# Dst-order passes of a four-layer graph network on blocks of 128 nodes in place of 256

## The chip, the core and the metric

One core of a Trainium2 chip runs the whole kernel. The metric is the device time of one execution in microseconds; the program before was timed in three runs. Five engines work beside each other, each through its own list of instructions in order: PE (TensorE), DVE (VectorE), ACT (ScalarE), POOL (GpSimd) and SP (SyncE), and they meet by semaphores. "PEld" is the weight load of TensorE, which the profile lists apart from the matmul.

## The reference

A graph of 6250 nodes (128 features each, f32) and 100000 edges, which are sorted by `dst` on entry. Four layers are applied, each to a normalized copy `h` of `x`, and added to `x`:

```python
edge_index = jnp.stack([src, dst])
h = jnp.maximum(_layernorm(x, axis=-1), 0.0)
x = x + _L0_gnn_ref(src, edge_type_200, dst, h, ...)       # 3 sums over edges by src, weighted; then softmax over all edges, sum
h = jnp.maximum(_layernorm(x, axis=-1), 0.0)
x = x + _L1_gnn_ref(h, edge_index, W, att_src, att_dst, bias)   # GAT: 8 heads, softmax over the edges of one dst, sum by dst
h = jnp.maximum(_layernorm(x, axis=-1), 0.0)
x = x + _L2_gnn_ref(h, edge_index, edge_attr_128, ...)     # segment_sum(x_nei[src] + edge_attr @ W.T, dst) / degree
h = jnp.maximum(_layernorm(x, axis=-1), 0.0)
x = x + _L3_gnn_ref(h, edge_index, edge_type_2, ...)       # segment_sum(one of two linear maps of X[src] by type, dst)
```

The work that counts is the segment sums: 128 floats of each of 100000 edges are added to the row of the edge's node, three times by `src` with a weight (layer 0), once more by `src` with the softmax, and by `dst` for `edge_attr`, the GAT layer, the mean layer and the typed layer.

## The kernel before

**A step.** A pass goes over the edges in tiles of 128. One step fetches the 128 rows of its tile, builds a one-hot matrix (128 edges x 256 nodes of a window, true where the edge's node is that column), and multiplies: PE has the fetched rows (128 x 128) as weights and the one-hot as the moving operand, and leaves 128 features x 256 nodes in PSUM. DVE adds that to the window's columns in an accumulator that holds all nodes (25 windows of `WN` = 256 columns). The number of the window is read from a table into a register for each step, so a tile lies in one window alone; where a window ends inside a tile the edges are tiled again from there. A pass has about 781 tiles of edges and some for the windows: 806 to 816 steps.

**The passes in order, with their place in the profiled execution** (us from the span's start):

- Preparation, to 346. DVE counts edges by window with one pass over all edge keys for each of the 25 windows (L458), works out where each tile starts (L497 and L499, a pair of operations for each window), and waits for records that POOL has scattered.
- ATTR, 346 to 1196, 808 steps in dst order. SP loads the rows of `edge_attr` by plain DMA (L1810). Meanwhile POOL scatters one record for each edge to put the edges into src order, 800 indirect DMAs (L1675).
- A normalization, then S0, S1, S2 from 1379 to 4943, 806 steps each in src order with weights, and SCORES, 5030 to 6276, in src order. From here on POOL fetches the rows of each step by an indirect DMA (a gather, L1696; L1712 in SCORES) into a ring of 16 tiles (33 in SCORES).
- GAT, 6468 to 7922, dst order, 816 steps in 51 groups of 16, ring of 48 tiles, gathers L1724.
- MEAN, 8015 to 9289, dst order, 808 steps; every 16 steps one extra product of 128 nodes is made (`own_term`: three matmuls L1177 to L1179 on PE, L582 and L584 on DVE).
- TYPED, 9429 to 10600, dst order, 808 steps; then the output.

**A step of the row passes** (ATTR, S0 to S2, MEAN, TYPED; `sum_pass` on DVE and on PE). DVE builds the one-hot `OH` (L604, or L601 with a weight) up to four steps ahead, and two instructions later adds the product of the step before last (L613). PE (L1184) waits for the one-hot, for the gathered rows and for the add that frees its PSUM bank. One f32 matmul is two MATMUL records and two LDWEIGHTS records in the trace. POOL (L1696) waits for `s_mm` of sixteen steps before, then issues its gather; nothing else stands in its queue.

**A step of GAT.** DVE makes the one-hot in bf16 (L991); PE transposes its two halves (L1356, L1357); ACT copies the transposed form out (L1574); PE looks up the attention terms of the edges' nodes by two matmuls of 24 columns (L1370). For each group of 16 steps a chain of 26 small DVE operations, seven PE steps and some on ACT works out the running maximum of each node and a factor by which old sums are rescaled (`rescale`, L981 and L983, once a group). ACT copies the one-hot to f32 (L1584), DVE multiplies the gathered rows by the attention (L998), PE forms the sums with the one-hot's halves as weights and the rows (146 columns: 128 features and 18 sums) as moving operand (L1380, L1381), and DVE adds 292 columns to the accumulator (L1014). The lookup side runs 33 steps ahead of the sums (`LAG1`), each engine's list being written out step by step in one loop.

Of the kernel before, what the change touches and what calls it, by code (L numbers as in the profile page):

```python
# [5 lines left out]
ALU = mybir.AluOpType  # L6
ACT = mybir.ActivationFunctionType
F32 = mybir.dt.float32
BF16 = mybir.dt.bfloat16
# [15 lines left out]
NTL = (E + NW * 142) // 128  # L25
# [7 lines left out]
NL1 = 816  # L33
# [18 lines left out]
def program(nc, x, src, dst, edge_attr_128, edge_type_2, edge_type_200,  # L52
# [5 lines left out]
    with ctx:  # L58
# [129 lines left out]
        def slot(k, dt=I32):  # L188
            v = RA[0:EP, k * EC:(k + 1) * EC]
            return v if dt is F32 else v.bitcast(dt)  # L190
# [19 lines left out]
        cnt1 = ST[:, 352:352 + NW]  # L210
# [36 lines left out]
        NER, NBR, NBB, KLR = RC[0:1, 1408:2224], RC[0:1, 2224:3040], RC[0:1, 3040:3856], WE0[0:1, 0:816]  # L247
        TR17, V17 = ST[0:1, 0:136], ST[0:1, 136:272]
        F17 = [ST[0:1, 272:408], ST[0:1, 408:544]]
        CFR = RC[0:1, 3856:3984]  # L250
        TRB, VBR = OH[0:1, 3, 0:128], OH[0:1, 3, 128:256]
        FBR, CBR = WE0[0:1, 0:128], WE0[0:1, 128:256]
        OHR, OHN = WE0[0:1, 256:512], WE0[0:1, 512:768]
        R18, DR = ST[0:1, 544:562], ST[0:1, 562:570]
        F18 = ST[:, 576:612].rearrange("p (a k) -> p a k", k=18)
# [48 lines left out]
        def window(e, regs, tab, t):  # L304
            if t % 16 == 0:
                e.load(regs, tab[0:1, t:t + 16])  # L306
            return e.snap(regs[t % 16], min_val=0, max_val=NW - 1)
# [4 lines left out]
        def _(v):  # L312
# [138 lines left out]
            tot1, nt1, cum1, st1, sh1 = (ST[:, 384 + 32 * k:384 + 32 * k + NW] for k in range(5))  # L451
            v.tensor_scalar(wi, slot(1), 8, None, ALU.arith_shift_right).then_inc(prep.sem, prep.one())
# [3 lines left out]
            for b in range(NW):  # L456
# [5 lines left out]
            v.tensor_copy(tot1, PS[2][:, 0:NW]).then_inc(prep.sem, prep.one())  # L462
            ti, al1 = SI[:, 8:8 + NW], ST[:, 592:592 + NW]
            own_done(prep)
            v.tensor_tensor_scan(st1, ONES[:, 0:NW], tot1, 0.0, ALU.mult, ALU.add).then_inc(prep.sem, prep.one())
            own_done(prep)
            v.tensor_copy(ti, st1).then_inc(prep.sem, prep.one())
            own_done(prep)
            v.tensor_scalar(ti, ti, 4, 4, ALU.arith_shift_right, ALU.logical_shift_left).then_inc(prep.sem, prep.one())
            own_done(prep)  # L470
            v.tensor_copy(al1, ti).then_inc(prep.sem, prep.one())
            v.tensor_copy(nt1[:, 0:1], st1[:, 0:1]).then_inc(prep.sem, prep.one())
            own_done(prep)
            v.tensor_tensor(nt1[:, 1:NW], st1[:, 1:NW], al1[:, 0:NW - 1], ALU.subtract).then_inc(prep.sem, prep.one())
            own_done(prep)
            v.tensor_scalar(ti, nt1, 127.0, None, ALU.add).then_inc(prep.sem, prep.one())
            own_done(prep)
# [1417 lines left out]
```

## Time and profile before

| | us |
|---|---|
| runs of the kernel before, median (lowest, highest) | 10542.12 (10536.25, 10543.48) |
| the profiled execution | 10618.11 |
| its span | 10616.3 |
| PE busy, PEld busy | 6277.0, 3729.0 |
| DVE busy | 6150.0 |
| POOL busy | 6440.6 |
| ACT busy | 1211.9 |
| DMA moved | 486.58 MB, mean 46 GB/s |

The profiled execution has its own time, 0.7% over the median. "Busy" is the time in which an engine executes; PE and PEld overlap. No engine is busy for more than 61% of the span, and a share of the whole is a mean over ten stages that differ, so the rows further on are read pass by pass.

### The profile page before, as it was taken

How to read it: one execution, taken by the hardware profiler on the slowest of the kernel's cores; microseconds unless marked ns; L12 is line 12 of the kernel's file. 1: busy time of each engine (PE TensorE's matmuls, PEld its weight loads, DVE VectorE, ACT ScalarE, POOL GpSimd, SP SyncE). 2: the span in 40 equal slices, each digit the busy share in tenths (PEclk: the TensorE clock that was granted, in tenths of full speed). 3: DMA queues.
4: the chain of work that ended last, by engine and by line, in shares of the span. 5: the costliest groups of instructions: out<-in, count | busy, mean ns of one | idle time of the engine just before them, and what ended most of it. 6: DMA issues, size and time to landing. Idle time of an engine off the chain costs nothing. (4 is left out here: it accounts for less than half of the span.)

```text
span 10616.3 us, 114972 instructions
## 1 busy us (share of the span) xinstructions
PE 6277.0 (59%) x20679; PEld 3729.0 (35%) x20679; DVE 6150.0 (58%) x20621; ACT 1211.9 (11%) x3342; POOL 6440.6 (61%) x6535
## 2 busy tenths in 40 slices
PE   0577446666555565555666666777764444575555
PEld 0233222223333333333333334666652333343333
DVE  6666457776545445555666675666675444434444
ACT  0000000000000000001333333444430000010000
POOL 3777766665666656665566635555545656536665
PEclk9988667667666666667666666777776777766666
DMA  2223211112111121112111111111111111211112
GB/s 40 52 63 64 58 39 45 45 46 53 46 46 46 46 54 46 46 46 52 42 43 43 43 39 40 39 40 40 40 26 59 43 42 43 41 48 46 46 46 54
DMA packets 392309, 486.58 MB, mean 46 GB/s; under 512 B 134290, under 2 KB 297942, under 8 KB 391350
## 3 DMA queue, kind: packets, MB, share of 16 engines
q0 software_dynamic: 206816, 377.82, 15.2%
q1 hardware_dynamic: 181770, 99.99, 3.3%
q8 instruction: 201, 3.29, 0.1%
q14 instruction: 502, 4.11, 0.1%
q10 hardware_dynamic: 3020, 1.36, 0.1%
HBM read 443.16 MB, written 37.86 MB: 45 GB/s over the span
## 5 line engine op out<-in xcount | busy, mean ns | idle before, releaser
L1184 PE MATMUL PS<-OH,RING 128*128 128x256 f32 x9684 | 3937.6, 537 | 2834.0 <-DVE OH L604 992.3
L1184 PEld LDWEIGHTS PS<-OH,RING 128*128 128x128 f32 x9684 | 2100.7, 251 | 4659.7 <-DVE OH L601 1525.6
L1696 POOL DMA_INDIRECT RING<-TAB,IDX x2418 | 2315.4, 958 | 1252.9 <-issue 626.4
L613 DVE TENSOR_TENSOR RA<-RA,PS 128x256 f32 x2418 | 1007.7, 417 | 1432.3 <-PE PS L1184 584.6
L613 DVE TENSOR_TENSOR RB<-RB,PS 128x256 f32 x2424 | 1018.8, 420 | 1109.9 <-PE PS L1184 443.0
L1712 POOL DMA_INDIRECT RING<-TABQ,IDX x806 | 784.1, 973 | 549.3 <-PE PS L1270 246.4
L1675 POOL DMA_INDIRECT REC<-RC x800 | 953.7, 1192 | 254.5 <-issue 242.5
L1696 POOL DMA_INDIRECT RING<-TABM,IDX x808 | 769.7, 953 | 543.6 <-issue 200.8
L1696 POOL DMA_INDIRECT RING<-TABN,IDX x808 | 768.1, 951 | 540.5 <-PE PS L1184 244.2
L601 DVE TENSOR_SCALAR OH<-IOTA,KEY,WE 128x256 f32<-128x256 f32 x2418 | 1023.9, 424 | 102.8 <-ACT RA L1492 45.7
L1270 PE MATMUL PS<-OH,RING 128*128 128x256 f32 x1612 | 759.6, 600 | 411.6 <-ACT OH L1516 234.7
L1724 POOL DMA_INDIRECT RING<-TABG,IDX x544 | 536.4, 986 | 540.9 <-PE PS L1381 310.2
L1270 PEld LDWEIGHTS PS<-OH,RING 128*128 128x128 f32 x1612 | 360.3, 272 | 753.7 <-ACT OH L1516 475.6
L604 DVE TENSOR_SCALAR OH<-IOTA,KEY 128x256 f32<-128x256 f32 x1616 | 579.8, 359 | 36.8 <-issue 36.7
L1014 DVE TENSOR_TENSOR RB<-RB,PS 128x292 f32 x816 | 370.1, 454 | 270.2 <-PE PS L1381 233.9
L1516 ACT ACTIVATE OH<-OHB,SC 128x256 f32<-128x256 bf16 x806 | 408.2, 506 | 769.0 <-DVE OHB L763 520.4
L712 DVE SCALAR_TENSOR_TENSOR RC<-IOTA,KEY,RB 128x256 f32<-128x256 f32 x806 | 386.3, 480 | 153.6 <-issue 101.9
L1574 ACT ACTIVATE OHT<-PS 128x256 bf16<-128x256 bf16 x816 | 312.3, 383 | 864.2 <-PE PS L1357 710.4
L776 DVE TENSOR_TENSOR RA<-RA,PS 128x256 f32 x732 | 303.5, 415 | 175.7 <-issue 132.1
L1724 POOL DMA_INDIRECT RC<-TABG,IDX x272 | 265.7, 977 | 226.2 <-PE PS L1381 143.6
L1380 PE MATMUL PS<-RING,OH 128*128 128x146 f32 x1088 | 355.9, 419 | 47.1 <-ACT OH L1584 24.1
L573 DVE SCALAR_TENSOR_TENSOR RC<-IOTA,SC,RELB 128x200 f32<-128x200 f32 x806 | 337.4, 419 | 0.0
(371 smaller groups left out, 6427.8 us busy)
## 6 DMA issues: line engine op xcount, KB each, us to landing
RING<-in_edge_attr_dram SPq DMA_DIRECT2D x808, 64.0 KB
RING<-TAB,IDX POOLq DMA_INDIRECT x2418
RING<-TABN,IDX POOLq DMA_INDIRECT x808
RING<-TABM,IDX POOLq DMA_INDIRECT x808
RING<-TABQ,IDX POOLq DMA_INDIRECT x806
REC<-RC POOLq DMA_INDIRECT x800
TAB<-HN SPq DMA_DIRECT2D x18, 512.0 KB, 3.4
RING<-TABG,IDX POOLq DMA_INDIRECT x544
```

Source lines behind the costliest of these rows:

```text
L601: v.tensor_scalar(OH[:, t % 4, :], IOTA[:, :], key[:, t:t + 1], WE0[:, t:t + 1], ALU.is_equal, ALU.mult).then_inc(s_oh, 1)
L604: v.tensor_scalar(OH[:, t % 4, :], IOTA[:, :], key[:, t:t + 1], None, ALU.is_equal).then_inc(s_oh, 1)
L613: v.tensor_tensor(sl, sl, PS[k % 4][:, 0:WN], ALU.add).then_inc(s_ad, 1)
L712: v.scalar_tensor_tensor(out=junk[:, t % 2, :], in0=IOTA[:, :], scalar=KEY0[:, t:t + 1], in1=PB[:, bass.ds(w * WN, WN)], op0=ALU.is_equal, ...
L1014: v.tensor_tensor(sl, sl, PS[a % 3][:, 0:292], ALU.add).then_inc(s_ab, 1)
L1184: t_.matmul(PS[t % 4][:, 0:WN], GD[:, t % 16, :], OH[:, t % 4, :], start=True, stop=True).then_inc(s_mm, 1)
L1270: t_.matmul(PS[a % 4][:, 0:WN], RG0[:, a % (3 * GS), 0:128], OH[:, a % 4, :], start=True, stop=True).then_inc(s_mm0, 1)
L1516: a_.activation(OH[:, a % 4, :], OHB[:, a % 4, :], ACT.Copy, scale=S0[:, a:a + 1]).then_inc(s_oh0, 1)
L1675: p.indirect_dma_start(REC0, bass.IndirectOffsetOnAxis(ap=posi0[:, c:c + 1], axis=0), v0[:, c:c + 1], None).then_inc(s_put[c % 8], 16)
L1696: p.indirect_dma_start(GD[:, t % 16, :], None, table, bass.IndirectOffsetOnAxis(ap=idx[:, t:t + 1], axis=0)).then_inc(s_ring[t % 16], 16)
L1712: p.indirect_dma_start(RG0[:, s, :], None, TABQ, bass.IndirectOffsetOnAxis(ap=IDX0[:, t:t + 1], axis=0)).then_inc(s_ring[t % 16], 16)
L1724: p.indirect_dma_start(rows_of(t)[:, 0:136], None, TABG, bass.IndirectOffsetOnAxis(ap=IDX1[:, t:t + 1], axis=0)).then_inc(s_ring[t % 16], 16)
```

## The change

All passes in dst order (ATTR, GAT, MEAN, TYPED) take blocks of 128 nodes (`ND` = 49 blocks of `WD` = 128) in place of 25 windows of 256. The src-order passes keep their windows of 256.

- Steps: ATTR, MEAN and TYPED 808 to 830, GAT 816 to 832 (52 groups of 16). Tiles are cut at multiples of 128 edges now, and a tile in which a block ends is fetched again for the next block.
- In a row pass the one-hot, the matmul's moving operand and the add are 128 columns wide.
- In GAT a step has one transpose, one lookup matmul, one product matmul; the copies by ACT, the add (146) and the rescaling (128 + 18) are half as wide, and a factor needs two matmuls for four.
- In the preparation DVE counts 49 blocks for 25 windows, and the starts of tiles come from seven counting operations in place of 24 pairs.

```diff
+ND = 49
+WD = 128
-NTL = (E + NW * 142) // 128
+NTL = 830
-NL1 = 816
+NL1 = 832
...
-            for b in range(NW):
+            for b in range(ND):
                 v.wait_ge(prep.sem, prep.n)
                 v.tensor_scalar(msk[0], wk, float(b), None, ALU.is_equal, ALU.add,
                                 accum_out=cnt1[0:EP, b:b + 1]).then_inc(prep.sem, prep.one())
...
-            for b in range(1, NW):
-                v.wait_ge(prep.sem, prep.n)
-                v.tensor_scalar(tm, tf, cum1[:, b - 1:b], nt1[:, b - 1:b], ALU.is_ge, ALU.mult).then_inc(prep.sem, prep.one())
-                v.wait_ge(prep.sem, prep.n)
-                v.tensor_tensor(BTF, BTF, tm, ALU.add).then_inc(prep.sem, prep.one())
+            for k in range(NTB):
+                own_done(prep)
+                v.tensor_scalar(steps[:, 0:ND - 1], cum1[:, 0:ND - 1], tf[:, k:k + 1], None, ALU.is_le, ALU.add,
+                                accum_out=W1F[:, k:k + 1]).then_inc(prep.sem, prep.one())
...
-                            v.tensor_scalar(OH[:, t % 4, :], IOTA[:, :], key[:, t:t + 1], None,
+                            v.tensor_scalar(OH[:, t % 4, 0:WD], IOTA[:, 0:WD], key[:, t:t + 1], None,
                                             ALU.is_equal).then_inc(s_oh, 1)
...
-                        sl = acc[:, bass.ds(w * WN, WN)]
-                        v.tensor_tensor(sl, sl, PS[k % 4][:, 0:WN], ALU.add).then_inc(s_ad, 1)
+                        sl = acc[:, bass.ds(w * width, width)]
+                        v.tensor_tensor(sl, sl, PS[k % 4][:, 0:width], ALU.add).then_inc(s_ad, 1)
...
-                    t_.matmul(PS[t % 4][:, 0:WN], GD[:, t % 16, :], OH[:, t % 4, :], start=True, stop=True).then_inc(s_mm, 1)
+                    t_.matmul(PS[t % 4][:, 0:width], GD[:, t % 16, :], OH[:, t % 4, 0:width], start=True, stop=True).then_inc(s_mm, 1)
...
-                    t_.transpose(pb[:, 0:128], OBR[:, t % 51, 0:128], IDENTB[:, :])
-                    t_.transpose(pb[:, 128:256], OBR[:, t % 51, 128:256], IDENTB[:, :]).then_inc(s_tp, 1)
+                    t_.transpose(pb, OBR[:, t % 51, 0:WD], IDENTB[:, :]).then_inc(s_tp, 1)
...
-                    t_.matmul(PS[a % 3][:, 0:146], OH[:, a % 3, 0:128], rows_of(a), start=True, stop=True)
-                    t_.matmul(PS[a % 3][:, 146:292], OH[:, a % 3, 128:256], rows_of(a), start=True, stop=True).then_inc(s_mb, 1)
+                    t_.matmul(PS[a % 3][:, 0:146], OH[:, a % 3, 0:WD], rows_of(a), start=True, stop=True).then_inc(s_mb, 1)
...
-                    v.tensor_tensor(sl, sl, PS[a % 3][:, 0:292], ALU.add).then_inc(s_ab, 1)
+                    v.tensor_tensor(sl, sl, PS[a % 3][:, 0:146], ALU.add).then_inc(s_ab, 1)
```

PE in the steady state of GAT: the lookup and the sums of one step, the transposes of the next, and the chain's matmuls for a factor (L1346 and L1347; AD is the table of attention terms). Before:

```order
L1370 ISA
L1370 MATMUL PS<-AD,OHT 128x24
L1370 ISA
L1370 MATMUL PS<-AD,OHT 128x24
L1380 MATMUL PS<-RING,OH 128x146
L1381 MATMUL PS<-RING,OH 128x146
L1356 MATMUL PS<-IDENTB,RA 128x128
L1357 MATMUL PS<-IDENTB,RA 128x128
L1346 MATMUL PS<-ONES,WE 128x18
L1347 MATMUL PS<-ST,WE 128x18
L1346 MATMUL PS<-ONES,WE 128x18
L1347 MATMUL PS<-ST,WE 128x18
```

and the same place after the change:

```order
L1354 ISA
L1354 MATMUL PS<-AD,OHT 128x24
L1362 MATMUL PS<-RING,OH 128x146
L1342 MATMUL PS<-IDENTB,RA 128x128
L1333 MATMUL PS<-ONES,WE 128x18
L1334 MATMUL PS<-ST,WE 128x18
```

The order of the kinds stays, and each pair is one instruction now. DVE in GAT at the end of a group, where old sums are rescaled (RB is the accumulator, ST the factors), before:

```order
L998 TENSOR_TENSOR RING<-RING 128x128
L894 SCALAR_TENSOR_TENSOR RC<-RC 128x128
L306 TENSOR_LOAD WTAB
L981 ISA
L981 TENSOR_TENSOR RB<-RB,ST 128x2x128
L983 ISA
L983 TENSOR_TENSOR RB<-RB,ST 128x2x18
L1014 TENSOR_TENSOR RB<-RB,PS 128x292
```

and after:

```order
L986 TENSOR_TENSOR RING<-RING 128x128
L882 SCALAR_TENSOR_TENSOR RC<-RC 128x128
L308 TENSOR_LOAD WTAB
L969 ISA
L969 TENSOR_TENSOR RB<-RB,ST 128x128
L971 ISA
L971 TENSOR_TENSOR RB<-RB,ST 128x18
L1002 TENSOR_TENSOR RB<-RB,PS 128x146
```

Nothing moved on DVE here; the same instructions are narrower. In MEAN and TYPED, too, each engine has the same instructions for a step as before.

## Rows read from the trace of the kernel before

**Rows 1.** Windows by pass: length; busy of PE, PEld, DVE, ACT, POOL; clock, DMA share.

```profile
346.00:1196.00 850.00, 595.85 (x1616) 306.81 (x1616) 582.31 (x1617) 0.00 (x0) 676.93 (x569) 0.86 0.30 64
...
5030.00:6276.00 1246.00, 799.53 (x1831) 385.98 (x1831) 856.72 (x3665) 427.00 (x986) 744.82 (x765) 0.65 0.18 42
...
6476.00:7878.00 1402.00, 1098.43 (x7180) 935.60 (x7178) 969.05 (x3662) 588.64 (x1929) 749.38 (x763) 0.75 0.18 39
8028.00:9289.00 1261.00, 624.66 (x1909) 391.33 (x1907) 568.19 (x1710) 0.00 (x0) 758.63 (x799) 0.72 0.17 42
9439.00:10599.00 1160.00, 660.77 (x1616) 359.70 (x1614) 542.93 (x1613) 0.00 (x0) 762.36 (x801) 0.68 0.19 46
```

**Rows 2.** Windows of line L1696 alone, POOL gathers of the MEAN and TYPED passes.

```profile
8015.00:9278.00 1263.00, 768.10 (x808) 0.72 0.18 45
9429.00:10591.00 1162.00, 769.70 (x808) 0.68 0.18 46
```

**Rows 3.** Page, costliest groups: the matmul of the row passes and its weight load.

```profile
L1184 PE MATMUL PS<-OH,RING 128*128 128x256 f32 x9684 | 3937.6, 537 | 2834.0 <-DVE OH L604 992.3
L1184 PEld LDWEIGHTS PS<-OH,RING 128*128 128x128 f32 x9684 | 2100.7, 251 | 4659.7 <-DVE OH L601 1525.6
```

**Rows 4.** Timeline of POOL in TYPED, two pauses; 14 gathers stand between them.

```profile
9879.40 0.95 POOL L1696 DMA_INDIRECT RING<-TABM,IDX  x1 [3.05 <-remote]
...
9899.45 0.95 POOL L1696 DMA_INDIRECT RING<-TABM,IDX  x1 [1.46 <-remote]
```

**Rows 5.** Timeline of DVE in TYPED: two steps of the fast phase, two slow.

```profile
9885.81 0.42 DVE L613 TENSOR_TENSOR RB<-RB,PS 128x256 f32 x1
9886.14 0.35 DVE L604 TENSOR_SCALAR OH<-IOTA,KEY 128x256 f32<-128x256 f32 x1
9886.44 0.42 DVE L613 TENSOR_TENSOR RB<-RB,PS 128x256 f32 x1
...
9891.63 0.42 DVE L613 TENSOR_TENSOR RB<-RB,PS 128x256 f32 x1 [2.15 <-PE PS L1184]
...
9895.12 0.42 DVE L613 TENSOR_TENSOR RB<-RB,PS 128x256 f32 x1 [2.74 <-remote]
```

**Rows 6.** MEAN: waits of the whole run, then timeline of DVE and of POOL.

```profile
DVE HN L582 <- remote: 476.6, 49, 12.2
...
8500.00 0.35 DVE L582 TENSOR_SCALAR HN<-PS,RDEG 128x128 f32<-128x128 f32 x1 [10.12 <-remote]
8500.39 0.29 DVE L584 TENSOR_TENSOR HN<-HN,PS 128x128 f32<-128x128 f32 x1
...
8502.49 0.94 POOL L1696 DMA_INDIRECT RING<-TABN,IDX  x1 [4.87 <-PE PS L1184]
```

**Rows 7.** GAT: windows of line L1014, then groups by form of 6476 to 7878.

```profile
6467.00:7922.00 1455.00, 369.95 (x816) 0.75 0.17 38
...
L1724 POOL DMA_INDIRECT RING<-TABG,IDX x507 | 498.8, 984 | 417.6 <-PE PS L1381 278.3 <-issue 137.9 <-remote 1.4
L1014 DVE TENSOR_TENSOR RB<-RB,PS 128x292 f32 x771 | 349.5, 453 | 263.7 <-PE PS L1381 228.5 <-remote 15.5 <-issue 10.9
...
L991 DVE TENSOR_SCALAR RA<-IOTAB,KEY 128x256 bf16<-128x256 bf16 x770 | 219.1, 285 | 0.1
...
L1380 PEld LDWEIGHTS PS<-RING,OH 128*128 128x128 f32 x1028 | 204.9, 249 | 51.4 <-issue 45.6 <-DVE RING L998 4.4
```

**Rows 8.** ATTR: timeline of SP and of POOL, waits of the whole run.

```profile
700.58 29.13 SPq L1810 DMA_DIRECT2D RING<-in_edge_attr_dram  x27
...
1360.85 1.19 POOL L1675 DMA_INDIRECT REC<-RC  x1 [0.30 <-issue]
...
DVE RC L519 <- DMA RC<-REC: 139.6, 1, 139.6
...
DVE HN L519 <- DMA RC<-RECX,SI: 98.9, 1, 98.9
```

**Rows 9.** Groups by form of DVE before 346 us (preparation).

```profile
L458 DVE TENSOR_SCALAR_CACHE_REDUCE RC<-RING 125x800 f32<-125x800 f32 x25 | 24.6, 986 | 0.9
```

More of the change, by code:

```diff
@@ L448, in _ @@
             v.tensor_copy(TWI[:, 0:NTB], W0F).then_inc(prep.sem, prep.one("tw0"))
-            tot1, nt1, cum1, st1, sh1 = (ST[:, 384 + 32 * k:384 + 32 * k + NW] for k in range(5))
-            v.tensor_scalar(wi, slot(1), 8, None, ALU.arith_shift_right).then_inc(prep.sem, prep.one())
+            tot1, st1, cum1, steps = (ST[:, 64 * k:64 * k + ND] for k in range(4))
+            v.tensor_scalar(wi, slot(1), 7, None, ALU.arith_shift_right).then_inc(prep.sem, prep.one())
             own_done(prep)
@@ new lines, in _ @@
+            for a, b, di in ((0, 33, ti), (33, 48, IOI[:, 0:15])):
+                own_done(prep)
+                v.tensor_copy(di, st1[:, a:b]).then_inc(prep.sem, prep.one())
+                own_done(prep)
+                v.tensor_scalar(di, di, 7, None, ALU.arith_shift_right).then_inc(prep.sem, prep.one())
+                own_done(prep)
+                v.tensor_copy(cum1[:, a:b], di).then_inc(prep.sem, prep.one())
+            own_done(prep)
+            v.tensor_tensor(cum1[:, 0:ND - 1], cum1[:, 0:ND - 1], IOTA[:, 1:ND], ALU.add).then_inc(prep.sem, prep.one())
@@ L470, in _ @@
             own_done(prep)
[L471 to L477, printed above, removed]
-            v.tensor_scalar(ti, ti, 7, None, ALU.arith_shift_right).then_inc(prep.sem, prep.one())
@@ L587, in sum_pass @@
                 n, base = ROW_PASSES[i], before[i]
+                width, blocks = (WN, NW) if weighted else (WD, ND)
                 for t in range(n + 2):
@@ L607, in sum_pass @@
                         k = t - 2
[L608 removed]
+                        w = window(v, regs, tab, k, blocks)
                         v.wait_ge(s_mm, base + k + 1)
@@ L961, in chain_step @@
                         v.wait_ge(s_scaled, c)
-                    v.tensor_copy(ST[:, 576:612], PS[7][:, 416:452]).then_inc(chain.sem, chain.one(("fac", c)))
+                    v.tensor_copy(F18, PS[7][:, 416:434]).then_inc(chain.sem, chain.one(("fac", c)))
             def chain_part(t, part):
@@ L1170, in sum_pass @@
                 n, base = ROW_PASSES[i], before[i]
+                width = WN if SUM0 <= i < SCORES else WD
                 for t in range(n):
```

99 lines of the change are left out of this document (39 added, 60 removed).

## The prediction

> **What bounds the kernel now.** I read the windows by pass first, since no engine is busy for more than 61% of the whole. The reader should see that the four dst-order passes have four different limits.
>
> ATTR [rows 1, 8]: DVE (582 us) and PE (596 us) are busy for some 70% of 850 us. SP issues a load each 29.13/27 = 1.08 us, and 808 steps in 850 us are 1.05 each, so SP's issuing is the pace. It isn't on the path: POOL's scatter of the records runs until 1360.85 + 1.19 = 1362.0, 166 us after ATTR's end at 1196, and S0 can't begin before; DVE waits 139.6 us for the records (`DVE RC L519 <- DMA RC<-REC`).
>
> MEAN and TYPED [rows 1, 2]: 1263/808 = 1.563 and 1162/808 = 1.438 us a step, with DVE and PE busy for about half. POOL's gather takes 0.95 us and 0.30 until the next; 15 of them take 9899.45 - 1.46 - 9879.40 = 18.59 us [rows 4], so call the floor 1.25 us a gather. POOL pauses for 3.05 us once in 15 or so, because it waits for `s_mm` of sixteen steps before: 15 x 1.25 + 3.05 is 21.8 us, or 1.45 a gather, which agrees. The ring is full at such a pause and PE slow: adds come 3.5 us apart (9891.63 to 9895.12), though for the fast phase ahead of them a step takes 9886.44 - 9885.81 = 0.63 us [rows 5]. So PE alternates between a fast phase of about 10 us (9879.40 to 9889.5, where the wait of the slow add begins) and a slow one, in which a step takes 3.5 us with rows and one-hots there. What makes PE slow I can't name; it sets in after POOL has issued without a pause for some time, and ends when POOL pauses. MEAN adds its own terms: DVE waits at L582 49 times, 476.6 us in all, and the POOL pause there is 4.87 us [rows 6].
>
> GAT [rows 1, 7]: 816 adds in 1455 us, 1.783 a step. POOL's gather is 0.984 + 0.30 = 1.29. DVE is busy for 969.05/771 = 1.26 us of each step, PE for 1.42; DVE waits 228.5 us for L1381, which is 0.30 a step. No slow phase of the kind above is to be seen; here the work itself, on DVE and PE in turn, is the limit.
>
> **The change part by part.** The sum is made against the profiled execution of 10618.11 us.
>
> *Preparation and ATTR: 0.* 24 more counts of 0.986 us [rows 9] and their readouts are about 25 us; less L497, which goes (10.8 us in 24), they leave +14 at most. They stand ahead of DVE's wait of 98.9 us for the records of the first scatters [rows 8], which swallows them. ATTR's 22 more steps at 1.05 are +23. Cover: 166 us until the scatter's end. A narrower one-hot doesn't help either, since SP is the pace. Were the cover gone, it would cost up to 37 us. Bounds 0 and 0.
>
> *GAT.* DVE: L1014 goes from 292 to 146 columns. An operation of this kind takes 0.42 us at 256 columns [rows 5] and 0.29 at 128 (L584, rows 6), which makes about 0.31 at 146, -0.145 from 0.453. L991 at 0.285 for 256 loses an estimated 0.07 by the same slope, halved for bf16. Rescale and the chain's two one-hots lose 0.4 us in 16 steps. Together -0.23 a step. PE: half of the product, transposes and lookups goes; that pays where DVE waits for L1381, of whose 0.30 I take half, -0.14. So 1.783 - 0.37 = 1.41, if nothing else comes up. But POOL then issues for 1.29/1.41 = 91% of the time, against 72% now, and passes with such a share show the slow phase: SCORES, the one with the most work beside the gathers, does 765 gathers in 1246 us, 1.63 [rows 1]. I take 1.48, nearer to the work than to SCORES. 832 x 1.48 = 1231, **-224**. Bounds: the gather's floor, 832 x 1.29 = 1073, -382; nothing gained a step, 832 x 1.783 = 1484, +29.
>
> *TYPED.* A step of the fast phase is DVE's one-hot and add, 0.63 now; each loses 0.13 at most (0.42 to 0.29), and by the overlap in these rows a step loses about 0.13: 0.50. The slow phase is unchanged in my forecast, 3.5 us a step. Then over a fast phase of 10 us, POOL issues 8 and PE does some 13 steps (0.63 to 0.85 each), the lead falls by 5, and comes back at 1/1.25 - 1/3.5 = 0.51 a us in 10 us; with the pause this is 23 us for 16 gathers, 1.44 as measured. With steps of 0.55 PE does 18, the lead falls by 10 and comes back in 19 us: 32 us for 23 gathers, 1.39. 830 x 1.39 = 1154, **-8**: the 22 steps more (32 us) eat the gain. Bounds: 830 x 1.25 = 1038, -124; 830 x 1.438 = 1194, +32.
>
> *MEAN.* The same, with 49 own terms. Now they cost (1.563 - 1.438) x 808 = 101 us, 2.06 each, or 0.12 a step. Part of DVE's wait for them lies in the slow phase anyway, and the lead has more room, so I take 0.08: 1.47. 830 x 1.47 = 1220, **-43**. Bounds: 1038, -225; 830 x 1.563 = 1297, +34.
>
> Gathers from memory: 22 + 22 + 16 more; they're in the counts of steps. S0 to S2, SCORES, normalizations and output have no edit.
>
> A weight load takes 249 ns with 146 moving columns and 251 with 256 [rows 3, 7], so PE's share of a step doesn't halve with the columns; in MEAN and TYPED a step has the same two loads, and only the matmuls (537 ns a record at 256) shrink.
>
> **Sum:** -224 - 8 - 43 = -275; 10618 - 275 = 10343 for an execution like the profiled one. The median of the runs is 0.7% lower, so 10542 - 275 x 10542/10618 = **10269, say 10270**.
>
> **The rivals.**
>
> *B, the slow phase goes with PE's work in columns, and POOL becomes the limit.* For it: 1.563 and 1.438 a step differ by about what the own terms add in columns (16 x 256 + 3 x 128 columns in 16 x 1.563 = 25.0 us, against 256 in 1.438: 179 and 178 a us). If halving the columns ends the slow phase, MEAN and TYPED come down to 1.25 (-225, -124), GAT to 1.41 (832 x 1.41 = 1173, -282). Sum -631: 9915. Against it: PE is idle in the slow phase, so nothing there is short of columns. There is one more way to this end. POOL's gathers might be held back by DVE: every L1696 in rows 4 and 6 shows 0.94 or 0.95, though around 9899.45 DVE stands idle and in the fast phase it is always busy, so the rows give this nothing, and the floor stays at 1.25. The Trainium skill, page "SBUF — State Buffer", box on the "DVE blocks DMA" trap, says that some two-port operations of VectorE lock GpSimd out of the port through which it writes DMA descriptors. By that rule narrower one-hots and adds would make each gather shorter than 0.95, and the three passes could end below even this rival; the trace doesn't agree with it here.
>
> *C, MEAN and TYPED keep their time a step.* If the slow phase is set by POOL alone (so many gathers, then a pause), a faster PE only waits longer. 22 more steps each cost +34 and +32; GAT stays at -224. Sum -158: 10385. For it: PE has half of its time free in these passes already. It and the forecast share GAT.
>
> *D, slower: the slow phase comes into GAT.* With GAT's work at 1.41 and POOL issuing for 91% of the time, PE might stall as it does in MEAN. It decides from the point where GAT's steps take (1455 - 66)/832 = 1.67 us or more, with MEAN and TYPED as in C; at 1.783 the sum is +29 + 34 + 32 = +95: 10636. Against it: SCORES, with its stalls, has 1.63; MEAN, with the worst, 1.563.
>
> *Same.* A GAT step between 1.64 and 1.70 with C.
>
> **How the numbers follow.** Forecast 0.45, with a range of its own of 10150 to 10340; B 0.22; C 0.22; D 0.08; within 0.2% 0.03. Faster: 0.45 + 0.22 + 0.22 = 0.89. The range goes from 9890, just under B, to 10450, over C with GAT at 1.56, and leaves out D, the same case, and a tail of B where GAT too is at its floor: about 0.2 with what I didn't think of. 0.2% (21 us) is about what a measurement of this kernel can tell from no change.
>
> **What would show it.** ATTR ends some 23 to 37 us later with S0's start where it was: then the zero is right. GAT, 832 adds: near 1231 us is the forecast, 1173 says that no slow phase came, over 1390 is D. TYPED near 1154 us with POOL's pauses further apart is the forecast; 1038 with hardly a pause is B; 1194 with the pauses where they are is C. MEAN in the same way at 1220, 1038 and 1297. The waits at L582 tell if own terms became cheaper. The prediction is wrong where the slow phase answers to something else that the change moves, for instance to how many semaphore updates a us meet at PE.

## The result

| | us |
|---|---|
| before, median of 4 runs (lowest, highest) | 10542.8 (10536.25, 10550.8) |
| after, median of 4 runs (lowest, highest) | 10410.51 (10399.24, 10417.02) |
| ratio, 95% interval | 0.9873 (0.9856 to 0.989) |
| after, profiled execution, its span | 10415.44, 10413.7 |

The change is faster by 1.3%, 132 us by the medians, and the interval leaves out 1. The forecast was 272 us. The windows of the passes in the trace of the changed kernel (length; busy of PE, PEld, DVE, ACT, POOL; clock, DMA share), answering to [rows 1]:

```profile
346.00:1025.00 679.00, 534.31 (x1654) 400.59 (x1652) 438.78 (x1653) 0.00 (x0) 540.86 (x454) 0.51 0.36 81
...
6418.00:7713.00 1295.00, 951.43 (x4122) 683.03 (x4122) 875.10 (x3878) 449.01 (x2032) 761.82 (x783) 0.50 0.19 43
7819.00:9066.00 1247.00, 550.76 (x1953) 436.22 (x1951) 435.91 (x1755) 0.00 (x0) 777.89 (x821) 0.55 0.17 44
9213.00:10397.00 1184.00, 552.43 (x1654) 393.25 (x1655) 410.03 (x1657) 0.00 (x0) 778.60 (x822) 0.53 0.18 46
```

DVE's busy time fell as the widths say, in MEAN from 568 to 436 us and in TYPED from 543 to 410. The passes hardly followed: MEAN 1247 for 1261 us, TYPED 1184 for 1160. GAT gave the gain. And one column moved that the prediction doesn't speak of: the granted clock of PE fell from 0.75 to 0.50 in GAT, which is the lower of its two levels (1.2 GHz) all through, and from 0.72 and 0.68 to 0.55 and 0.53 in the two passes behind it.

The forms of GAT's main operations, and its adds in windows of line L1002 (832 in 1297 us, 1.56 a step; [rows 7] had 816 in 1455):

```profile
L1002 DVE TENSOR_TENSOR RB<-RB,PS 128x146 f32 x830 | 251.8, 303 | 256.4 <-PE PS L1362 174.3 <-issue 45.5 <-remote 23.8
L979 DVE TENSOR_SCALAR RA<-IOTAB,KEY 128x128 bf16<-128x128 bf16 x796 | 200.4, 252 | 3.0 <-issue 2.3 <-ACT OH L1565 0.4
...
L1362 PE MATMUL PS<-RING,OH 128*128 128x146 f32 x1116 | 454.0, 517 | 41.0 <-issue 39.6 <-DVE RB L1002 1.2
...
6417.00:7714.00 1297.00, 252.40 (x832) 0.50 0.19 43
```

The add costs 0.303 us (the estimate was 0.31), the one-hot 0.252 (0.215 expected). The product matmul, though its shape is unchanged, takes 517 ns a record for 419 (L1380 before). That goes with the clock: where it is 0.85 with the same product (k2, below), the record takes 374.

The adds of TYPED in DVE's timeline, answering to [rows 5]:

```profile
9709.92 0.29 DVE L601 TENSOR_TENSOR RB<-RB,PS 128x128 f32 x1
...
9710.42 0.29 DVE L601 TENSOR_TENSOR RB<-RB,PS 128x128 f32 x1
...
9713.15 0.29 DVE L601 TENSOR_TENSOR RB<-RB,PS 128x128 f32 x1 [0.96 <-PE PS L1173]
...
9715.97 0.29 DVE L601 TENSOR_TENSOR RB<-RB,PS 128x128 f32 x1 [2.27 <-PE PS L1173]
...
9718.13 0.29 DVE L601 TENSOR_TENSOR RB<-RB,PS 128x128 f32 x1 [1.67 <-PE PS L1173]
...
9722.34 0.29 DVE L601 TENSOR_TENSOR RB<-RB,PS 128x128 f32 x1 [3.73 <-issue]
...
9727.23 0.29 DVE L601 TENSOR_TENSOR RB<-RB,PS 128x128 f32 x1 [4.40 <-remote]
```

A fast step is 0.50 us, as forecast. The slow phase is still there, with steps of 1.4 to 4.9 us. The fast stretch ahead of it, from 9705.80 to 9711.70, has eleven steps in 6 us; the prediction had some 13 steps in 10 us.

PE isn't slow in the slow phase. The same stretch in the timeline of all engines has the matmul between the adds of 9718.13 and 9722.34, and k3, a later run of the changed kernel where no slow phase is, has one too (its add follows at 8604.76):

```profile
9718.67 0.80 PE L1173 MATMUL PS<-OH,RING 128*128 128x128 f32 x2 [1.36 <-issue]
```

```profile
8603.85 0.76 PE L1173 MATMUL PS<-OH,RING 128*128 128x128 f32 x2 [0.40 <-issue]
```

The matmul ends at 9719.47 and its add starts 2.87 us later; in k3 it is 0.15 us. The traces also record when a semaphore rises. For the matmuls of TYPED it rises 14 ns after the end of the matmul nearly always in k3 (828 records), and more than 0.6 us after the end of the latest matmul in half of the 699 records of the changed kernel, in the latest over 4 us. DVE's own semaphores rise 11 ns after the instruction in both traces. So what comes late is the word that the result is there. (The ends of matmuls are modelled in a trace, but in the same way in both.)

The preparation and ATTR are the zero that was forecast: DVE now waits 307.9 us for POOL's records, which are as late as before ([rows 8]: 1360.85). That ATTR takes 679 us for 850 isn't the change's doing: the unchanged kernel took 670 us for it in a second trace (h1, below), and the pass after it begins between 1378 and 1381 us in all three. SP's pace of 1.05 us a step is no fixed figure, then.

```profile
1358.30 1.19 POOL L1656 DMA_INDIRECT REC<-RC  x1 [0.30 <-issue]
...
DVE RC L506 <- DMA RC<-REC: 307.9, 1, 307.9
```

### The profile page after: what moved, and what is told of

Same layout as the page of the kernel before. It is cut to its first block and busy times, and to the rows that moved or that the text cites. A ratio compares the mean times of both kernels' runs of the same rounds, so it can differ in the third digit from the quotient of the medians.

```text
span 10413.7 us, 108515 instructions
## 1 busy us (share of the span) xinstructions
PE 5831.4 (56%) x17424; PEld 3587.3 (34%) x17424; DVE 5604.8 (54%) x20814; ACT 1045.8 (10%) x3382; POOL 6484.6 (62%) x6595
## 5 line engine op out<-in xcount | busy, mean ns | idle before, releaser
L1173 PE MATMUL PS<-OH,RING 128*128 128x128 f32 (+1 forms) x9816 | 3661.3, 511 | 2892.0 <-issue 932.3
L1173 PEld LDWEIGHTS PS<-OH,RING 128*128 128x128 f32 x9816 | 2231.3, 279 | 4321.6 <-issue 1810.0
L601 DVE TENSOR_TENSOR RB<-RB,PS 128x128 f32 x2490 | 719.0, 289 | 1347.6 <-PE PS L1173 710.1
L1656 POOL DMA_INDIRECT REC<-RC x800 | 953.3, 1192 | 252.7 <-issue 242.8
L1259 PE MATMUL PS<-OH,RING 128*128 128x256 f32 x1612 | 756.0, 600 | 394.4 <-ACT OH L1497 240.4
L1259 PEld LDWEIGHTS PS<-OH,RING 128*128 128x128 f32 x1612 | 362.3, 272 | 727.5 <-ACT OH L1497 456.4
L592 DVE TENSOR_SCALAR OH<-IOTA,KEY 128x128 f32<-128x128 f32 x1660 | 494.2, 298 | 37.4 <-issue 36.2
L1362 PE MATMUL PS<-RING,OH 128*128 128x146 f32 x1120 | 455.6, 517 | 41.5 <-issue 39.6
L1002 DVE TENSOR_TENSOR RB<-RB,PS 128x146 f32 x832 | 252.4, 303 | 256.7 <-PE PS L1362 174.3
L1362 PEld LDWEIGHTS PS<-RING,OH 128*128 128x128 f32 x1120 | 296.4, 325 | 53.1 <-issue 49.8
```

What stands on the lines that cost most here:

```text
L592: v.tensor_scalar(OH[:, t % 4, 0:WD], IOTA[:, 0:WD], key[:, t:t + 1], None, ALU.is_equal).then_inc(s_oh, 1)
L601: v.tensor_tensor(sl, sl, PS[k % 4][:, 0:width], ALU.add).then_inc(s_ad, 1)
L1173: t_.matmul(PS[t % 4][:, 0:width], GD[:, t % 16, :], OH[:, t % 4, 0:width], start=True, stop=True).then_inc(s_mm, 1)
L1259: t_.matmul(PS[a % 4][:, 0:WN], RG0[:, a % (3 * GS), 0:128], OH[:, a % 4, :], start=True, stop=True).then_inc(s_mm0, 1)
L1362: t_.matmul(PS[a % 3][:, 0:146], OH[:, a % 3, 0:WD], rows_of(a), start=True, stop=True).then_inc(s_mb, 1)
L1656: p.indirect_dma_start(REC0, bass.IndirectOffsetOnAxis(ap=posi0[:, c:c + 1], axis=0), v0[:, c:c + 1], None).then_inc(s_put[c % 8], 16)
```

## The experiments

The theory after the result: a step of MEAN and TYPED is set by something in which the width has no part (rival C for these two), and GAT lost part of its gain to the colder clock. The rivals: the width counts but the clock takes it back; or the stalls have one cause that a small edit could take away. All kernels but h1, f0 and k3 are the changed one with an edit. Several edits in different passes share a run, since a pass can be read by itself: by the window from its first add to its last, in which the x is the adds and the figure behind it the clock. Each such profile is one execution, and a pass untouched by the edits differs between the executions with slow phases (MEAN 1247 to 1269 us, GAT 1297 to 1320, ATTR by far more), so passes are compared within one chip where they can be. For chips see "The chips differ".

**e1: GAT's products and transposes twice, as before, on PE.** The second lookup matmul and the chain's two more matmuls for a factor aren't back: PE is busy for 1087 us in GAT, against 952 in the changed kernel and 1133 in h1.

```diff
+                    t_.transpose(PS[3 + t % 2][:, 64:128].bitcast(BF16), OBR[:, t % 51, 0:WD], IDENTB[:, :])
                     t_.transpose(pb, OBR[:, t % 51, 0:WD], IDENTB[:, :]).then_inc(s_tp, 1)
...
+                    t_.matmul(PS[a % 3][:, 146:292], OH[:, a % 3, 0:WD], rows_of(a), start=True, stop=True)
                     t_.matmul(PS[a % 3][:, 0:146], OH[:, a % 3, 0:WD], rows_of(a), start=True, stop=True).then_inc(s_mb, 1)
```

> The changed kernel, but GAT's product and transpose are each done twice, as before the change (the second result isn't used), so PE has before's work and DVE and ACT have the narrow operations. GAT takes 1296 us in the changed kernel (832 steps, 1.56 each), at a granted clock of 0.50, against 0.75 before. Theory A (the clock that PE lost is what kept GAT above my 1.41): the granted clock comes back to about 0.75 and GAT takes less than 1296, down to 1200. Rival B (PE's amount of work is what counts, the clock only follows): GAT gets slower, 1330 to 1450. Rival C (PE is beside the path, GAT goes by POOL and the slow phase): 1290 to 1310, whatever the clock.

**e2: MEAN and TYPED at 256.** One-hot, matmul and add with `WN` for `WD` in these passes. The upper columns turned out not to be zeros where a tile holds edges of the next block; these are counted twice, so the sums aren't the layers'. The times are those of the width.

> The changed kernel with one-hot, matmul and add 256 columns wide again in MEAN and TYPED, over the same 830 tiles (the upper 128 columns are zeros). MEAN takes 1246.5 us and TYPED 1183.6 in the changed kernel. If the time a step is set by what POOL and the slow phase do, whatever the width (rival C of the prediction): TYPED stays within 10 us of 1184 to 1194 (830 x 1.437 = 1193) and MEAN goes to 830 x 1.5625 = 1297 at most. If width counted, but was eaten by the colder clock, TYPED gets slower than 1200.

GAT's adds in e1, then those of e2 (GAT there is untouched, on the same chip), then MEAN and TYPED of e2:

```profile
6481.00:7874.00 1393.00, 252.65 (x832) 0.74 0.18 41
```

```profile
6481.00:7800.00 1319.00, 252.00 (x831) 0.50 0.18 43
...
7905.00:9198.00 1293.00, 348.66 (x830) 0.73 0.16 42
9344.00:10539.00 1195.00, 348.76 (x829) 0.67 0.17 46
```

With this work GAT is 74 us longer, at a clock of 0.74 for 0.50: rival B of the expectation. PE's work counts, and the fast clock doesn't make up for it. TYPED at 256 columns takes 1195 us, against 1191 at 128 in e1: the width is worth 4 us in 830 steps. MEAN takes 1293 against 1260 and 1269 (e1, e3): 24 to 33 us. MEAN is longer than TYPED by 98 us in e2 and by 69 in e1, so nearly all of this lies with the own terms.

**e3: a ring of 32 tiles for TYPED**, and **e4: POOL waits for the add.**

```diff
-                    if t >= 16:
-                        p.wait_ge(s_mm, base + t - 15)
+                    depth = 32 if i == TYPED else 16
+                    if depth > 16 and t >= 16:
+                        landed(p, i, t - 16)
+                    if t >= depth:
+                        p.wait_ge(s_mm, base + t - depth + 1)
```

The edit also makes POOL wait for the landing of the gather 16 before, since two tiles now share a semaphore.

> The changed kernel with a ring of 32 tiles in place of 16 for TYPED alone: POOL may be 32 gathers ahead. If the fast phase comes only when POOL pauses because the ring is full, and a pause costs some 3 us, pauses come half as often and TYPED goes from 1184 us to 830 x (1.25 + 0.19/2) = 1116 us. If the slow phase is a matter of the rate at which PE's results can be told while POOL issues, a deeper ring only lengthens both phases and TYPED stays at 1184, within 15.

> The changed kernel, but POOL waits for the add (s_ad) of sixteen steps before in place of the matmul's semaphore (s_mm) in S0 to S2, MEAN and TYPED, so that DVE alone waits for s_mm. In the trace of the changed kernel s_mm is raised up to 10 us after its matmul was issued in the slow phase of TYPED. If that lateness comes from two engines waiting for one semaphore, it goes: TYPED falls from 1184 toward 1038 and S1 from 1156 toward 1010. If not, both stay within 15 us.

Windows of the adds: TYPED in e3; then S1 and TYPED in e4.

```profile
9316.00:10532.00 1216.00, 239.24 (x830) 0.52 0.17 45
```

```profile
2583.00:3753.00 1170.00, 337.39 (x806) 0.68 0.17 45
9262.00:10459.00 1197.00, 238.89 (x830) 0.51 0.18 46
```

The deeper ring makes TYPED longer by 25 us (1191 in e1), which neither branch of the expectation had. So a full ring isn't what is short, and my picture, in which a pause of POOL is paid once for each filling of the ring, is wrong. Gathers start more than 1.6 us apart 99 times in e3 and 131 times in e1, and what they lose by it is 147 us in both: fewer pauses, each longer.

Who waits for `s_mm` doesn't matter in S1 and TYPED. In MEAN it may: the pass took 1237 us in e4, outside the 1247 to 1269 of the others, and DVE's wait for the own terms was 157.2 us there, against 474.9 in the trace of the changed kernel. That is one execution, and no run followed it up.

**f1: one update for two steps** (`then_inc(s_mm, 2)` at each second matmul), **f2: gathers of 256 bytes a row in TYPED** (half of the features are fetched, so the sum isn't the layer's), **f3: GAT's old widths for DVE's one-hot (256) and add (292)** (the rescaling stays narrow), and **f0: the changed kernel again.**

> The changed kernel, but PE raises s_mm once for two steps (by 2, at the second matmul) in S0 to S2, MEAN and TYPED. On the chip of the runs e1 to e4 S1 takes 1163 to 1168 us and TYPED 1184 to 1196. If telling a result is what is slow (one update of PE for each 0.7 us or more while POOL issues), half the updates let PE keep up, and S1 goes toward POOL's floor of 1010 us, TYPED toward 1040. If PE's matmul itself is slow then, or the pace is set by something else, both stay within 20 us.

> The changed kernel, but each row gathered in TYPED is 256 bytes in place of 512 (half of the features are fetched, so TYPED's sum is not the layer's). Same number of gathers and descriptors, half of the bytes. If the slow phase comes from bytes moved by the gathers, TYPED drops well below 1184, to 1040 to 1120; if it goes by the number of gathers or of descriptors, it stays within 15 us of the other runs of this job.

> The changed kernel, but in GAT DVE makes the one-hot 256 wide and adds 292 columns again (the upper half adds zeros); PE and ACT keep the narrow work. It is the other half of e1, where PE had its old work: GAT there took 1391 us against 1318 for the changed kernel's GAT on the same chip. The prediction gave DVE 0.23 us a step and PE 0.14. If that is right, GAT takes 1318 + 832 x 0.21 = 1490 us here; with both back it would be 832 x 1.78 = 1484, of which PE is 73, so if the parts add up it is 1411 us; if DVE is beside the path, it stays at 1318.

> The changed kernel itself, on the chip of this job, timed against the kernel before: 0.985 to 0.989 as on record. Its passes in this profile are what the other runs of the job are compared with: GAT 1296 to 1318, MEAN 1236 to 1269, TYPED 1184 to 1196, S1 1156 to 1168.

f0 was 0.99 of before (0.9883 to 0.9917). Windows of its adds in GAT and TYPED; then TYPED in f1, TYPED in f2, GAT in f3:

```profile
6444.00:7764.00 1320.00, 252.01 (x831) 0.50 0.17 43
...
9273.00:10464.00 1191.00, 238.76 (x829) 0.53 0.16 46
```

```profile
9294.00:10484.00 1190.00, 239.50 (x830) 0.50 0.16 46
```

```profile
9284.00:10476.00 1192.00, 239.03 (x830) 0.52 0.10 23
```

```profile
6447.00:7763.00 1316.00, 377.06 (x831) 0.50 0.17 43
```

1191, 1190, 1192: neither the number of updates nor the bytes (23 GB/s for 46) is in it. S1 in f1 took 1163 us for f0's 1161. And f3 is the hardest miss: DVE is busy for 377 us in place of 252 in its add alone, and GAT takes 1316 us, 4 less than with the narrow one. The add and the one-hot, to which the forecast gave 0.215 us a step (179 us), are beside the path when they alone are wide.

**h1: the kernel before again; h2: three edits in three passes.** S1: the wait for the landing moves from PE to DVE. TYPED: one-hot as weights, gathered rows as moving operand (the sum stands transposed and isn't the layer's). GAT: ACT copies 256 columns, DVE's one-hot is 256 wide. The same edits were in **g1** (TYPED and GAT) and **g2** (S1; in TYPED gathers write to slots that PE doesn't read, so the sum isn't the layer's), on a chip that has no slow phase.

```diff
+                    if i == TYPED:
+                        t_.matmul(PS[t % 4][:, 0:width], OH[:, t % 4, 0:width], GD[:, t % 16, :], start=True, stop=True).then_inc(s_mm, 1)
```

> The changed kernel with two edits in different passes. TYPED: PE takes the one-hot as weights and the gathered rows as moving operand (as GAT does), so the sum stands transposed and isn't the layer's; same sizes, same steps. So far nothing that was changed in these passes (width, bytes, ring depth, number of updates, who waits) moved the 1.43 to 1.44 us a step. GAT has no slow phase, and there the gathered rows are the moving operand: if PE is slow at loading freshly gathered rows as weights while POOL issues, TYPED goes from 1190 toward POOL's floor of 1040; if not, it stays within 15. GAT: ACT copies 256 columns again and DVE's one-hot is 256 wide, PE and the add stay narrow. With PE's old work GAT took 1391 (e1), with DVE's 1315 (f3), with none 1319; before's steps would be 1484. If ACT's copies were the rest, GAT takes up to 1410 here; if the three only count together, 1319 to 1335.

> The changed kernel with two edits in different passes. S1: DVE waits for the landing of a step's rows before it makes the one-hot, and PE no longer waits for a semaphore that DMAs raise (in GAT it doesn't either). If this wait is what slows PE while gathers land, S1 goes from 1160 toward 1010 us; else it stays within 15. TYPED: the gathers write to slots 16 to 31 of the ring, and PE reads slots 0 to 15, which nothing writes (so the sum is not the layer's); the waits stay. If PE is slow because it reads rows that a DMA has just written or writes nearby, TYPED goes from 1190 toward 1040; else it stays within 15.

> The kernel before itself, for its profile on the chip of this job. The chips differ: on two of them a step of the row passes takes 1.44 us with or without the change, on a third (runs g1 and g2) 1.25 us with the changed kernel, which is POOL's pace, and no slow phase is there. If the job runs on a chip with slow phases: S1 1160 to 1168, GAT 1454 to 1475, MEAN 1261 to 1275, TYPED 1160 to 1175 us. If it runs on one without: S1 1008, TYPED 808 x 1.25 = 1010, MEAN 1010 to 1030, GAT 1120 to 1200; the changed kernel has 22 more steps there for MEAN and TYPED each and so is slower in these two by 22 x 1.25 = 28 us each.

> The changed kernel with the edits of g1 and g2 in three passes, for a chip with slow phases (g1 and g2 ran on one without, so they couldn't tell). S1: DVE waits for the landing of a step's rows, PE doesn't: 1160 if that wait is nothing, toward 1010 if it is what slows PE. TYPED: the one-hot is the weights and the gathered rows move (the sum stands transposed and isn't the layer's): 1190 if it doesn't matter which operand is gathered, toward 1040 if slow weight loads are the cause. GAT: ACT copies 256 columns, DVE's one-hot is 256 wide, PE and the add narrow: 1319 if ACT is beside the path, up to 1410 if ACT was the rest of the gain. On a chip without slow phases all three are as in g1 and g2 (1008, 1040, 1119).

S1 and TYPED in g1, on the chip without slow phases:

```profile
2423.00:3432.00 1009.00, 338.59 (x805) 0.58 0.19 53
8077.00:9118.00 1041.00, 238.95 (x830) 0.50 0.18 52
```

g1 and g2 say nothing on what the edits do to a slow phase: S1 takes 1009 us there with and without one, which is POOL's pace. Now h1, GAT (L1014), then S1, MEAN and TYPED (L613); and h2, S1 and TYPED, then GAT:

```profile
6415.00:7848.00 1433.00, 369.99 (x816) 0.75 0.16 39
...
2572.00:3725.00 1153.00, 336.18 (x806) 0.67 0.16 46
7954.00:9207.00 1253.00, 339.12 (x808) 0.73 0.16 42
9355.00:10507.00 1152.00, 339.66 (x807) 0.66 0.17 46
```

```profile
2579.00:3741.00 1162.00, 336.58 (x806) 0.62 0.16 46
9234.00:10418.00 1184.00, 238.98 (x830) 0.52 0.16 46
...
6426.00:7726.00 1300.00, 251.56 (x831) 0.50 0.17 43
```

S1 1162, TYPED 1184, GAT 1300, against 1156, 1184 and 1297 in the trace of the changed kernel, whose src-order passes agree with h1's to 7 us: none of the three edits matters. ACT's copies, too, are beside GAT's path when they and the one-hot alone are wide.

h1 gives the account that the recorded profile of before, some 80 us longer than the median, couldn't. Changed kernel against h1: GAT 1297 - 1433 = -136, MEAN 1247 - 1253 = -6, TYPED 1184 - 1152 = +32, together -110; the two executions took 10415.44 and 10525.25 us, which is -110 too. h2, on h1's own chip, gives nearly the same with edits that cost nothing: -133, +2, +32.

h1 also shows how much of GAT's step before was waiting for the late word. DVE's wait for the product there, and in k1, which has most of the same work on a chip without slow phases:

```profile
DVE RB L1014 <- PE PS L1381: 220.2, 270, 3.1
```

```profile
DVE RB L1003 <- PE PS L1366: 58.3, 165, 1.4
```

**i1, i2, i3, and k1: pace, lead, no gathers, the wide products, transposes, copies, one-hot and add back together, and a kept clock.** S1 in i1 and k1: POOL does a small memset and waits for it ahead of each gather. S2 in i1: POOL waits for the landing of the gather two before; S2 in k1 and S1 in i2: POOL at most 6 ahead. TYPED in i1 and k1 has no gathers (PE reads what lies in the ring, so the sum isn't the layer's). GAT in i1 and k1 has the edits of e1, f3 and h2 together; the second lookup, the two more matmuls for a factor and the wide rescaling are still missing, so it isn't all of before's work, as the expectations call it. MEAN in i2 has no own terms, so the layer's sum lacks them. i3, timed again as k2:

```diff
+                    for _ in range(2):
+                        t_.matmul(PS[3 + t % 2][:, 128:384], IDENTB[:, :], IOTAB[:, :], start=True, stop=True)
                     t_.transpose(pb, OBR[:, t % 51, 0:WD], IDENTB[:, :]).then_inc(s_tp, 1)
```

> The changed kernel with four edits in different passes. S1: POOL does a small memset and waits for it before each gather, so its gathers are some 1.5 us apart and not 1.25. If the slow phase needs gathers back to back, it goes and the pass takes what POOL takes, with adds evenly spaced; if stalls come whatever the pace, S1 gets longer than POOL's pace by as much as now (0.19 a step). S2: POOL waits for the landing of the gather two before: the same question with fewer transfers in flight; 1153 to 1160 if nothing changes. TYPED: no gathers, PE reads what lies in the ring (the sum isn't the layer's): 830 steps of the fast phase, 0.50 us each, are 415 us if stalls need POOL's gathers; if they come by themselves, 830 x 0.9 or more. GAT: all engines have their old widths back over the 832 steps (PE, DVE, ACT), which is before's work: 832 x 1.76 to 1.78 = 1462 to 1484 us; with PE's alone it was 1391 (e1), with DVE's alone 1315 (f3), with ACT's 1299 (h2). If the parts add up it would be 1391.

> The changed kernel with two edits. S1: POOL may be 6 gathers ahead and not 16. If a full ring is what ends a slow phase, pauses come after fewer gathers; a pause of 3 us for each 5 gathers would make S1 806 x (1.25 + 0.6) = 1490 us. If PE's stalls come as a fixed share of time, S1 stays near 1160 or up to 1250. MEAN: without the own terms (left out of the layer's sum). 830 x 1.43 = 1187 us if they cost what is left above TYPED's step, so 1247 - 1187 = 60 us for 49 of them, 1.2 each; my forecast had 0.08 a step, 66 us.

> The changed kernel with two extra bf16 matmuls of 256 columns in each step of GAT, ahead of the transpose, whose result nobody reads. They cost PE some 0.3 us a step and should bring its granted clock from 0.50 back toward 0.75. If the lost clock was what kept GAT at 1.56, GAT gets faster than 1296 to 1300 us in spite of them; if PE's work counts at any clock, it goes to 1330 to 1450.

> The changed kernel with four edits, for a chip with slow phases (the runs i1 to i3 ran on one without; there S1 with a memset ahead of each gather took 1152 us, TYPED without gathers 472, and GAT with all widths back 1195 against 1114). S1: memset before each gather, POOL's own pace 1.43: near 1152 us if the stalls need gathers at 1.25, 1250 or more if they come on top. S2: POOL at most 6 ahead: 1006 on the chip without, near 1155 if the lead is nothing, up to 1490 if every full ring costs 3 us. TYPED without gathers: 472 if the stalls need gathers, more if they come by themselves. GAT with all widths back: 1462 us, as before's steps on a chip like the recorded one; 1391 if only PE's part counted.

> The kernel of i3 (two matmuls that nobody reads in each GAT step), timed. On a chip without slow phases its GAT took 1090 us against 1114, at a clock of 0.83 against 0.50. On one with them: GAT 1296 to 1319 without the dummies; if the clock counts there too, 1270 to 1295 with them, and the kernel's ratio to before is 0.002 below that of k3; if PE's extra work is dearer there, 1320 to 1390 and a ratio above k3's.

> The changed kernel itself, timed beside k2 on the same chip: 0.985 to 0.992 of before on a chip with slow phases, 0.993 to 0.997 on one without (g1, g2, i1 and i2 beside before there gave 0.994 to 0.998 with edits that cost nothing there).

All six ran on chips without slow phases. GAT in k1, the changed kernel's (k3), with two idle matmuls (k2); then S1 and TYPED of i1:

```profile
5819.00:7008.00 1189.00, 375.78 (x832) 0.89 0.19 48
```

```profile
5671.00:6787.00 1116.00, 251.70 (x831) 0.50 0.20 51
```

```profile
5669.00:6751.00 1082.00, 248.85 (x831) 0.85 0.21 53
```

```profile
2426.00:3579.00 1153.00, 338.97 (x805) 0.51 0.18 46
8633.00:9106.00 473.00, 239.74 (x830) 0.79 0.00 1
```

There the work that k1 puts back is worth 73 us in GAT. k2 does more work than k3 and is faster by 34 us, with a product record of 374 ns for 517: the lower clock costs at least that, if the two matmuls act by nothing else, which no run separates. Timed, k2 is 0.9922 of before (0.9908 to 0.9935), k3 0.9954 (0.9941 to 0.9968). So k2 beats both kernels on such a chip; on one with slow phases it wasn't run. The Trainium skill, page "TensorE: Matmul & The Clock Gate", section "What's actually happening", says that the lower clock is the default and that activity lifts it; the trace agrees, 0.50 without the extra matmuls and 0.85 with them.

What k1 leaves out can be estimated. Before takes 43 us more than k3 on that chip, though its MEAN and TYPED have 22 gathers less each, 28 us at POOL's 1.25. If all else but GAT is equal, before's GAT takes 1116 + 43 + 55 = 1214 us, 1.49 a step, and all the narrow work is worth 832 x 1.49 - 1116 = some 120 us, of which k1 shows 73. The rest would be the lookup, the factors and the rescaling.

TYPED without gathers is 0.57 us a step (473/830), so PE and DVE need less than half of what a gather needs. Own terms cost nothing there: MEAN takes 1031 us in i2 without them, and 1029 in i1 and i3 on the same chip with them. A lead of 6 is enough: S1 1009 us in i2, S2 1008 in k1. With POOL's memset S1 took POOL's pace, 1153 us, and with the wait for the landing S2 in i1 1346, for 1008 (k3). Whether any of these would end the stalls on a chip that has them stays open.

## The chips differ

Before took 10622.77 us where e1 to e4 ran, 10589.88 with f, 10537.16 with h, and 9159.27, 9181.64 and 9176.75 us with g, i and k: 13% less, for one program. Each letter ran on a chip of its own, once, so a property of the chip can't be told from one of the occasion; "chip" stands for both here. The trace shows where the time goes. In k3 adds of TYPED come at POOL's pace and POOL never pauses:

```profile
8602.57 0.94 POOL L1677 DMA_INDIRECT RING<-TABM,IDX  x1 [0.30 <-issue]
8603.82 0.94 POOL L1677 DMA_INDIRECT RING<-TABM,IDX  x1 [0.30 <-PE PS L1173]
...
8603.60 0.29 DVE L601 TENSOR_TENSOR RB<-RB,PS 128x128 f32 x1 [0.78 <-PE PS L1173]
...
8604.76 0.29 DVE L601 TENSOR_TENSOR RB<-RB,PS 128x128 f32 x1 [0.68 <-PE PS L1173]
```

MEAN and TYPED take 1.25 us a step there, GAT 1.34. So the slow phase is no property of this program alone. What makes some chips show it isn't settled. One rival was left untested: the recording of the profile itself, from which every execution on record has its span and clock. The traces with slow phases miss many of their own semaphore records: for DVE's two semaphores in TYPED the changed kernel's has 304 and 341 of 830, k3's 827 and 830. Whether a kernel that isn't profiled has the slow phases isn't shown by any run.

## Why the prediction was wrong

**Preparation and ATTR, 0:** right. The 22 more steps and the 24 more counts went into the cover. The sign that I named for it, ATTR's end 23 to 37 us later, didn't come: it ended at 1025 us for 1196, and h1's at 1015.

Where the forecast of 275 us lost 165 against the traces (h1 to the changed kernel, 110): GAT 88, TYPED 40, MEAN 37.

**TYPED, -8, and the step that failed.** "Then over a fast phase of 10 us" and "With steps of 0.55 PE does 18" took the fast phase as a fixed length of time, and "The slow phase is unchanged in my forecast, 3.5 us a step" took the slow steps as fixed too. Neither held. In h1, 494 steps of TYPED took less than 0.9 us, 346 us together, and the other 313 took 2.57 us each; in the changed kernel it is 408 steps in 233 us, and 421 of 2.26 us each. What the short steps save, the long steps take back: the mean step stayed (1.426 us in h1, 1.427 in the changed kernel; 1195 and 1191 us for 830 steps at 256 and 128 columns, e2 and e1), and 22 more steps cost +32 us by h1, as rival C had it. That rival's mechanism, so many gathers and then a pause, isn't shown: e3's ring didn't change the time that pauses cost. e3 shows the same failure from the other side: the ring's picture gave 1116 us and it took 1216. Nor is PE slow, as the prediction has it: in the trace that it read, too, the matmul before the add of 9895.12 had ended at 9893.13.

**MEAN, -43:** -6 by h1. The step of 1.39 that it was built on is TYPED's, and failed with it. The part that was its own came out: the own terms were to cost 66 us for 101, and MEAN is longer than TYPED by 63 us in the changed kernel and by 101 in h1 (69 and 71 in e1 and f0). DVE's wait for them, which the prediction names as the sign, stayed all the same, 474.9 us for 476.6.

**GAT, -224: the sign and the place were right, the terms weren't.** It gave -136 (1.756 to 1.559 a step; forecast 1.48). The failed step is "here the work itself, on DVE and PE in turn, is the limit", with its 0.23 us for DVE. The DVE term measures 0 when its add and one-hot are taken by themselves (f3), and ACT's copies 0 (h2). PE's part, to which I gave 0.14, is 0.09 for the products and transposes (74/832, e1). GAT had its part of the slow phase, too, though the prediction saw none: of DVE's wait for L1381, 220.2 us in h1, k1 has 58.3. The product's semaphore rises more than 0.9 us after the latest product in a tenth of h1's 752 records, and 15 ns after it nearly always in k1. I had read DVE's busy share (1.26 of 1.78) as its place on the path; the wait for L1381 said whose turn it was.

The 16 steps more add 16 x 1.756 = 28, so the narrow work gave 164 us in all. 74 are the products' and transposes'. The other 90 are open: e1, f3 and h2 each widened a part alone, no edit brought back the second lookup, the factors or the rescaling, and no run on a chip with slow phases had the parts wide together. Two sizes in the sum were off besides: 0.145 + 0.07 + 0.025 is 0.24 and not 0.23, and SCORES' 1.63 divides its 1246 us by the 765 gathers that fell into them, though it has 806 steps in that time, 1.55 each. And 22 of the 224 belong to the execution that the rows came from, in which GAT took 1455 us for h1's 1433.

**What the sum left out: the clock.** I took half of the columns from PE in GAT and didn't ask what PE's clock would do. It fell from 0.75 to 0.50, where a matmul of the same shape takes 517 ns for 419. On chips without slow phases that is at least 34 us of GAT (k2, k3), if the two extra matmuls act by the clock alone; on the others it wasn't measured, and e1 has more work and more clock at once.

**Rival B** (slow phases go with PE's columns): false, e2. **D** (they come into GAT so that nothing is gained): GAT takes 1.56 where chips without slow phases have 1.34, so it pays for them, but it did so before the change too, and stayed below the 1.67 from which D decides. **The profiled execution** of before was 0.7% over the median, and I scaled that away over the whole sum. The excess isn't spread evenly: against h1 it is 40 us in S0 to S2, 22 in GAT, some 8 each in MEAN and TYPED.

**Open:** why the word of PE's results comes late in the slow phase. Width, bytes, number of updates, who waits, PE's wait for landings and the operand that is gathered were each changed without moving the 1.43 to 1.44 us; the deeper ring made it 1.465.

## What to carry to other kernels

A step that waits for something unnamed wasn't shortened here by making its operations smaller, and splitting blocks to make them smaller added steps, which were paid in full: count the steps first. Where fast and slow phases alternate, don't hold one fixed while the other changes before a run has shown it; the mean may be what is fixed. Look whether the engine is late or only the word of its result: compare the end of its instruction with the start of the one that waits. A busy share doesn't put an engine on the path; widening its part alone does or doesn't. And an edit that takes work off TensorE can take its clock as well; look at the granted clock of the stage and, if it is above the lower level, price the same matmuls at the lower one.

## What was unexpected of the hardware

- Chips of one kind run this program in 9160 to 9180 or in 10540 to 10620 us. On the slower ones the word of PE's results comes late in phases: a matmul that ended at 9719.47 is added at 9722.34, while DVE's semaphores are on time.
- These late adds keep to a grid. In TYPED of the changed kernel 92% of the 413 distances over 1.2 us lie within 0.06 us of a multiple of 0.70 us; in k3 16% do. Nothing here says why.
- 1.43 to 1.44 us a step held there in TYPED for rows of 256 and of 512 bytes, for 128 and 256 columns, and for one update a step or one for two.
- Two matmuls a step that nobody reads made a pass faster by 3% (1116 to 1082 us), with a granted clock of 0.85 for 0.50.
